# Down products of a two-layer attention and mixture-of-experts kernel: two fp32 passes replaced by three fp32r products of leading and trailing parts

## What is computed

```python
xn = ln(x, g_norm)
q = (xn @ Wq) ; k, v = split(xn @ Wkv)        # 16 heads of 64, one k/v head
q, k = l2norm(q) * q_scale, l2norm(k) * k_scale
attn = softmax(q @ k.T * 8 + bias, causal, masked)   # bias of a small network, plus a null key
x = x + ln(attn @ v @ Wout, g_out)

scores = softmax((x @ wt.T + g @ wg.T) / 2)   # 8 experts, the best 2 are kept, weights sum to 1
gp = leaky(x @ w_gate) ; up = x @ w_up         # per expert, 128 hidden units
y_all = (gp * up) @ w_down                     # per expert: the down products
y = sum of the two chosen y_all, weighted
p = (leaky(x @ sw_gate) * (x @ sw_up)) @ sw_down    # shared, 256 hidden units
x = x + y + p
```

## Time and profile before

| | |
|---|---|
| device time, 3 runs | 1133.45, 1135.3, 1136.15 us (median 1135.3) |
| device time of the profiled execution | 1139.32 us |
| its span, first to last instruction | 1137.4 us |
| TensorE matmul busy | 1028.3 us (90%), 7340 instructions |
| VectorE busy | 781.0 us (69%) |
| ScalarE busy | 526.0 us (46%) |
| GpSimd busy | 443.3 us (39%), 422 instructions |
| down products (L1460) | 640 instructions, mean 395 ns |
| granted TensorE clock, mean | 0.976 |
| round 4 (its expert transposes to the next ones) | 425.7 to 556.3 us |
| the tail | 1078.2 to 1137.4 us |

### The profile page before, as it was taken

The page is one execution under the profiler, slowest core; times in us unless marked ns, Lnnn a source line. Parts: engine busy times, 40 slices in busy tenths (PEclk is TensorE's granted clock), DMA queues, the critical chain, the costliest instruction groups (busy, mean ns, idle before and its releaser), DMA issues.

```text
span 1137.4 us, 22612 instructions
## 1 busy us (share of the span) xinstructions
PE 1028.3 (90%) x7340; PEld 843.4 (74%) x7340; DVE 781.0 (69%) x2538; ACT 526.0 (46%) x1563; POOL 443.3 (39%) x422
## 2 busy tenths in 40 slices
PE   2377899999999999899999999899998999999898
PEld 1265587777877788677877787777877778777777
DVE  6768858775687648775587747876597756866442
ACT  2048724663356614655255623565146642566111
POOL 3154414553435505453336424354145433355112
PEclk9688999999999999999999999999999999999999
DMA  5064411321123212321123111221113211232033
GB/s 203 19 177 158 150 38 56 104 85 57 40 80 98 66 40 74 103 66 38 58 91 96 59 55 58 92 68 65 59 56 103 84 38 33 81 103 65 20 104 119
DMA packets 40939, 89.89 MB, mean 79 GB/s; under 512 B 4128, under 2 KB 18976, under 8 KB 40304
## 3 DMA queue, kind: packets, MB, share of 16 engines
q1 hardware_dynamic: 40816, 88.29, 24.3%
HBM read 78.67 MB, written 11.70 MB: 79 GB/s over the span
## 4 chain that ended last, share of the span: by engine, by line
PE 66%; DVE 20%; issue 6%; ACT 5%; POOL 1%; DMA 1%; SPq 1%; DVEq 0%; ACTq 0%; POOLq 0%
PE psY L1460 11%; PE psO L1393 6%; PE psS L1363 5%; PE psG L63 4%; PE psG L65 4%; PE psG L64 4%; PE psT L1374 3%; PE psS L63 3%; PE psS L64 3%; DVE work L1042 3%; PE psS L65 3%; PE psS L1358 2%; PE psO L1396 2%; PE psT L63 2%; PE psT L65 2%
## 5 line engine op out<-in xcount | busy, mean ns | idle before, releaser
L552 POOL TENSOR_TENSOR work<-work,rden 128x514 f32<-128x514 f32 x128 | 134.3, 1049 | 329.1 <-DVE rden L1023 328.5
L1460 PE MATMUL psY<-Wd,H 128*128 128x256 f32 x640 | 166.7, 395 | 3.7 <-POOL H L566 3.7
L675 ACT ACTIVATE work<-work,low 128x257 f32<-128x257 f32 x256 | 128.3, 503 | 80.7 <-DVE low L1042 80.6
L63 PE MATMUL psG<-x1T_hi,Wgu 128*128 128x512 f32 x280 | 128.1, 458 | 11.7 <-ACT leaky L707 9.8
L1460 PEld LDWEIGHTS psY<-Wd,H 128*128 128x128 f32 x640 | 113.3, 189 | 32.3 <-issue 15.6
L1042 DVE CUSTOM_DVE_ANT_0 work<-psS,bias,null_s 128x256 f32<-128x256 f32 x256 | 113.0, 478 | 18.3 <-PE psS L1363 18.0
L1132 DVE SCALAR_TENSOR_TENSOR leaky<-leaky 128x512 f32<-128x512 f32 x80 | 55.6, 695 | 101.5 <-ACT leaky L707 100.5
L541 POOL TENSOR_TENSOR rq<-qss,neghalf 128x16 f32<-128x16 f32 x32 | 93.7, 2930 | 55.0 <-DVE qss L1017 55.0
L65 PE MATMUL psG<-x1T_lo,Wgu 128*128 128x512 f32 x280 | 110.3, 394 | 0.0
L64 PE MATMUL psG<-x1T_hi,Wgu 128*128 128x512 f32 x280 | 109.6, 391 | 0.0
L667 ACT ACTIVATE qT_hi<-psO 128x256 fp32r<-128x256 f32 x128 | 48.9, 382 | 108.8 <-PE psO L1396 107.7
(11 more groups left out here) (242 smaller groups left out, 2677.4 us busy)
## 6 DMA issues: line engine op xcount, KB each, us to landing
Wgu<-wexp SPq DMA_DIRECT2D x80, 512.0 KB, 3.5
Wb<-wscr SPq DMA_DIRECT2D x64, 256.0 KB, 3.7
wexp<-Wgu SPq DMA_DIRECT2D x10, 512.0 KB, 2.9
xin<-in_x SPq DMA_DIRECT2D x8, 512.0 KB, 4.1
xres<-in_x SPq DMA_DIRECT2D x8, 512.0 KB, 5.0
out<-work SPq DMA_DIRECT2D x8, 512.0 KB, 3.1
H<-in_wgu SPq DMA_DIRECT2D x10, 256.0 KB, 3.8
bscr<-bscr SPq DMA_DIRECT2D x1, 2048.0 KB, 13.0
```

The costliest lines, as they stand in the source:

```text
L63: te.matmul(dst, a_hi, b_hi, start=start, stop=False)
L552: pool.tensor_tensor(T1[sl][:, hs, :], T1[sl][:, hs, :], rden[sl][:, 1, hs].unsqueeze(2) .to_broadcast([P, 2, N + 1]), ALU.mult)
L675: act.activation(T1[sl][:, h, :], T1[sl][:, h, :], ACT.Exp, scale=-1.0, bias=low[sl][:, 1, h:h + 1], accum_out=den[sl][:, 1, h:h + 1])
L1460: mm = te.matmul(psY[:, t // 2, (t % 2) * D:(t % 2 + 1) * D], H[:, k % H_RING, t * P:(t + 1) * P], Wd[:, ORDER[k], :], start=(k == 0 and t ...
```

## The change

Each down product becomes three: leading by leading, trailing by leading, leading by trailing part. `Wd` is split once, in round 0: its four pieces are loaded behind the third expert weights into buffers that are free then (`wd_in`), ScalarE writes the leading parts and GpSimd subtracts for the trailing ones (`DOWN_SPLIT_AT`). `H` is split for each block: ScalarE's `lead` copies it to a leading part and GpSimd's `trail` subtracts; both write into `Hp`, a ring of two in the buffers of the transposed tokens `xnT`, which hold nothing in use then. `lead(k)` waits for the weighted (or shared) hidden values and for the down products of block k - 2; `trail(k)` for `lead(k)`; `down(k)` and the reuse of `H` for `trail(k)`. The down products of blocks 0 and 1, which stood ahead of step 0, go to steps 1, 3 and 4, and block 2 wholly into step 5. `WT` moves into unused rows of `PNT`, so the product with `PNT` takes 64 rows.

```diff
-DOWN_AT = {4: (2, FIRST), 5: (2, SECOND), 6: (3, FIRST), 7: (3, SECOND), 8: (4, WHOLE), 9: (5, FIRST), 10: (5, SECOND),
-           11: (6, FIRST), 12: (6, SECOND), 13: (7, FIRST), 14: (7, SECOND), 15: (8, FIRST), 16: (8, SECOND), 18: (9, WHOLE)}
+LEAD_AT = {3: 2, 4: 3, 5: 4, 7: 5, 9: 6, 11: 7, 13: 8, 15: 9}
+TRAIL_AT = {3: 2, 4: 3, 5: 4, 7: 5, 9: 6, 11: 7, 13: 8, 15: 9}
+DOWN_AT = {1: (0, WHOLE), 3: (1, FIRST), 4: (1, SECOND), 5: (2, WHOLE), 6: (3, FIRST), 7: (3, SECOND), 8: (4, WHOLE),
+           9: (5, FIRST), 10: (5, SECOND), 11: (6, FIRST), 12: (6, SECOND), 13: (7, FIRST), 14: (7, SECOND),
+           15: (8, FIRST), 16: (8, SECOND), 18: (9, WHOLE)}
+HP_RING = 2
+DOWN_PARTS = 4
+DOWN_SPLIT_AT = {7: 0, 9: 1, 10: 2, 11: 3}
...
+        wd_in = [(range(0, 4), Wb[:, :, :].rearrange("p b t -> p (b t)")), (range(4, 6), leaky[0][:]),
+                 (range(6, 8), leaky[1][:]), (range(8, 10), x1[:, 0:2, :].rearrange("p t d -> p (t d)"))]
...
 @block.sync
-            sp.dma_start(Wd[:], wdown).then_inc(ld_down.sem, 16)
...
             for e in range(BLOCKS + 2):
+                if e == H_RING:
+                    for blocks, raw in wd_in:
+                        sp.dma_start(raw, wdown[:, blocks[0]:blocks[-1] + 1, :].rearrange("p b d -> p (b d)")) \
+                            .then_inc(ld_down.sem, 16)
...
 @block.gpsimd (attention)
                     if t < POOL_TILES:
                         scale_q(pool, r, t, qn_pool)
+                    if t == 3 and moe is not None:
+                        trail(moe, 0)
+                        trail(moe, 1)
                 for n in range(ALL):
+                    if moe is not None and n in TRAIL_AT:
+                        trail(moe, TRAIL_AT[n])
                     if moe is not None and n in WEIGH_AT:
                         weigh(moe, WEIGH_AT[n])
+                    if moe is None and n in DOWN_SPLIT_AT:
+                        blocks, raw = wd_in[DOWN_SPLIT_AT[n]]
+                        hi, lo = (part[:, blocks[0]:blocks[-1] + 1, :].rearrange("p b d -> p (b d)") for part in Wd)
+                        pool.wait_ge(wd_lead.sem, DOWN_SPLIT_AT[n] + 1)
+                        pool.tensor_tensor(lo, raw, hi.bitcast(F32), ALU.subtract).then_inc(wd_trail.sem, 1)
...
+            def trail(m, k):
+                need(pool, hh_done, m, k + 1)
+                pool.tensor_tensor(Hp[1][:, k % HP_RING, :], H[:, k % H_RING, :], Hp[0][:, k % HP_RING, :].bitcast(F32),
+                                   ALU.subtract).then_inc(hl_done.sem, 1)
...
 (GpSimd's tail)
-            for k in range(SHARED, BLOCKS):
-                weigh(ROUNDS - 1, k)
+            for k in range(BLOCKS):
+                if k >= SHARED:
+                    weigh(ROUNDS - 1, k)
+                if k >= 1:
+                    trail(ROUNDS - 1, k - 1)
+            trail(ROUNDS - 1, BLOCKS - 1)
...
 @block.scalar (attention)
+                if moe is not None:
+                    lead(moe, 0)
                 for n in range(4):
                     turned_q(r, n)
                     if n == 1 and moe is not None:
                         take_gate(moe, 2)
+                        lead(moe, 1)
...
+                    if moe is not None and n in LEAD_AT:
+                        lead(moe, LEAD_AT[n])
+                    if moe is None and n in DOWN_SPLIT_AT:
+                        blocks, raw = wd_in[DOWN_SPLIT_AT[n]]
+                        act.wait_ge(ld_down.sem, 16 * DOWN_PARTS)
+                        act.activation(Wd[0][:, blocks[0]:blocks[-1] + 1, :].rearrange("p b d -> p (b d)"), raw,
+                                       ACT.Copy).then_inc(wd_lead.sem, 1)
                     if TURN_LAG <= n < ALL + TURN_LAG:
                         turned(r, n - TURN_LAG)
...
+            def lead(m, k):
+                if k < SHARED:
+                    need(act, h_done, m, k + 1)
+                else:
+                    need(act, hw_done, m, k + 1 - SHARED)
+                if k >= HP_RING:
+                    need(act, h_used, m, k + 1 - HP_RING)
+                act.activation(Hp[0][:, k % HP_RING, :], H[:, k % H_RING, :], ACT.Copy).then_inc(hh_done.sem, 1)
...
 (ScalarE's tail)
             for k in range(BLOCKS):
                 take_gate(ROUNDS - 1, k, True)
+                if k >= 2:
+                    lead(ROUNDS - 1, k - 2)
+            lead(ROUNDS - 1, BLOCKS - 2)
+            lead(ROUNDS - 1, BLOCKS - 1)
...
 @block.vector (hidden)
-                    need(dve, h_used, m, k + 1 - H_RING)
+                    need(dve, hl_done, m, k + 1 - H_RING)
...
 @block.tensor
                 if moe is not None:
                     up(moe, 2)
-                    down(moe, 0, WHOLE)
-                    down(moe, 1, WHOLE)
...
             def down(m, k, tiles):
-                if k < SHARED:
-                    need(te, h_done, m, k + 1)
-                else:
-                    need(te, hw_done, m, k + 1 - SHARED)
+                need(te, hl_done, m, k + 1)
...
-                    mm = te.matmul(psY[:, t // 2, (t % 2) * D:(t % 2 + 1) * D],
-                                   H[:, k % H_RING, t * P:(t + 1) * P], Wd[:, ORDER[k], :],
-                                   start=(k == 0 and t % 2 == 0), stop=(k == BLOCKS - 1), skip_group_check=True)
+                    for a, b in ((0, 0), (1, 0), (0, 1)):
+                        mm = te.matmul(psY[:, t // 2, (t % 2) * D:(t % 2 + 1) * D],
+                                       Hp[a][:, k % HP_RING, t * P:(t + 1) * P], Wd[b][:, ORDER[k], :],
+                                       start=(k == 0 and t % 2 == 0 and a + b == 0), stop=(k == BLOCKS - 1 and b == 1),
+                                       skip_group_check=True)
```

More of the change, by code:

```diff
@@ L140, in attention_moe @@
         Wout = [sb(f"Wout_{part}", [P, PAIRS, D], F32R) for part in PARTS]
-        Wd = sb("Wd", [P, BLOCKS, D])
+        Wd = [sb(f"Wd_{part}", [P, BLOCKS, D], F32R) for part in PARTS]
         Wt = sb("Wt", [P, KC, E])
@@ L202, in attention_moe @@
         Wb = sb("Wb", [P, WB_RING, TOK])
-        WT = sb("WT", [E, TOK])
+        Hp = xnT
+        WT = PNT[DH:DH + E, :]
         lg = sb("lg", [P, TILES, E])
@@ L352, in attention_moe @@
         hw_done = events("hw_done", E, 1)
+        hh_done = events("hh_done", BLOCKS)
+        hl_done = events("hl_done", BLOCKS)
+        wd_lead = events("wd_lead", 0)
+        wd_trail = events("wd_trail", 0)
         xnT_ps = events("xnT_ps", 2)
@@ L1342, in attention @@
                                  [part[:, p, :] for part in Wout], p == 0, False)
-                    te.matmul(dst, PNT[:, t * P:(t + 1) * P], Unull[:], start=False, stop=True) \
+                    te.matmul(dst, PNT[0:NULL_ROWS, t * P:(t + 1) * P], Unull[0:NULL_ROWS, :], start=False, stop=True) \
                         .then_inc(wo_ps.sem, 1)
@@ L1470, in _ @@
             te.wait_ge(w_trail.sem, 2)
-            te.wait_ge(ld_down.sem, 16)
             keys(0)
@@ L1474, in _ @@
             attention(0, None, 1)
+            te.wait_ge(wd_trail.sem, DOWN_PARTS)
             with te.Fori(1, ROUNDS - 1) as r:
```

5 lines of the change are left out of this document (3 added, 2 removed).

## The result

| | before | after |
|---|---|---|
| device time, median of 4 runs | 1134.38 us (1133.03 to 1136.15) | 1179.93 us (1179.89 to 1180.26) |
| profiled execution, span | 1139.32, 1137.4 us | 1179.89, 1177.8 us |
| program's start to the first expert transposes (round 0) | 165.0 | 173.3 |
| rounds 1 to 7 | 913.2 | 931.0 |
| tail | 59.2 | 73.5 |

What follows compares the result with a forecast made beforehand. The bound was priced by stage: TensorE in mid-round, VectorE's chain at round entries. TensorE -7, entries +13, step 11 +6, round 0 +4 and tail +13 made +29 on 1139.3; 1168 less 4 gave 1164 us, range 1150 to 1176.

Steps and rivals of the forecast that it cites:

- Direction: Whole kernel: the change makes it slower, chance 0.92.
- the tail (+13): Last token block's experts: down(1) waits 5.5 us, six periods grow from 4.46 to 5.7 us; +13 us (10 to 16).
- Entry of each round (+1.9): Seven round entries: two GpSimd subtractions hold off VectorE's router operations, +1.9 us each (0 to 2.1), +13 us in all.
- Nothing is gained there ... Price zero: Moving downs 0 and 1 from ahead of step 0 into steps 1, 3 and 4 neither gains nor costs.
- Step 11 (+0.9): VectorE's norm_x is held off by one more subtraction, placed in front: +0.9 us (0 to 1.2), six rounds, +6 us.
- TensorE's part from step 5 on (-1.0): Three down products replace two fp32 instructions: 1.0 us less a round (0.3 to 1.8), seven rounds, -7 us.
- Round 0 (+4): Splitting Wd loads ScalarE and GpSimd, and its loads delay the fourth expert-weight load: +4 us (1 to 7).
- less 4: Whole kernel: 4 us off the sum, since unprofiled runs' median is 4.0 us below the profiled execution.
- one subtraction only: Round entry: only one subtraction is in VectorE's way, 0.95 us a round, giving 1157 us; chance 0.15.
- no hold-off: Rounds: subtractions into fp32r tiles run beside VectorE without stopping it, giving 1145 us; chance 0.12.
- TensorE is the bound and the copies are hidden: Whole kernel, tail included: faster, 26 us less than 1135, giving 1109 us; chance 0.05.
- the clock falls in the tail: Tail: the stall before down(1) brings half clock speed for some 7 us more, giving 1171 us; chance 0.10.

Runs made afterwards that it cites:

- a_tail: Changed kernel, in the tail each subtraction ahead of the next block's weighting and each leading copy right behind the gate copy, one block earlier: 1167.3 us, ratio 1.0303.
- a_down_first2: Changed kernel, down products of blocks 0 and 1 ahead of step 0 again, block 2 still whole in step 5: 1174.3 us, ratio 1.0361.
- b_down_later: Kernel before, its fp32 down products of blocks 0 and 1 moved into steps 1 and 3, no copies or subtractions: 1141.6 us, ratio 1.0073.
- b_rows64: Kernel before, only the null product narrowed from 128 to 64 rows: 1147.4 us against 1135.4, ratio 1.0117.
- best5: Changed kernel, 128-row null product, downs 0 and 1 ahead of step 0, entry, step-11, tail and round-0 copies or subtractions rescheduled, down(7) whole in step 14: 1134.4 us, ratio 0.9991.
- a_rows128: Changed kernel, null product over all 128 rows again: 1173.2 us, ratio 1.0355.
- b_turn: Kernel before, the tail's routing weights transposed right behind gate(1) and copied behind the first gate copy: 1134.2 us, ratio 0.9991.
- a_round0_late: Changed kernel, Wd's loads behind the eighth expert-weight load and its split in steps 12 to 15 of round 0: 1175.4 us, ratio 1.0384.

## Why the prediction was wrong, point by point

- **Direction, and the tail (+13):** right. +14.3 in the profile, with period and place of down(1) as worked out; the last down ends 69.3 us into the tail (forecast 68.2). a_tail confirms the order as its cause. What the sum lacked is the first period, 7.16 us for 5.61, with the half-clock stretch in it.
- **Entry of each round (+1.9):** the mechanism and the size were right: 2.0 us, by a_down_first2. Missed was what TensorE does in that time.
- **"Nothing is gained there ... Price zero" for the downs of blocks 0 and 1:** this step failed. It asked only whether score(0) would come earlier, not what the idle that takes the place of 3.5 us of products does to the clock. It costs 0.3 to 0.5 us a round with a half-clock stretch of 3.4 us and 1.0 to 1.9 with one of 6.8, some 5 us together; b_down_later shows 8.2 us for the move alone. I had the clock as a rival in the tail, where the earlier trace rows showed it, and did not carry it to the place where the change made a new wait.
- **The null product over 64 rows:** the step that is missing, and the largest. The text on the change named it; the prediction put it at nothing, without a reason. By b_rows64 it is 12 us in the kernel before (10.4 to 16 by the interval); in the changed kernel the traces place 9.2 us.
- **Step 11 (+0.9):** the size was right: score(12) to score(13) takes 6.1 us after and 5.2 before; best5 takes it back. The order was misread: the subtraction comes behind the two normalization instructions. The size came out because norm_x is held off by a subtraction behind them as by one in front.
- **TensorE's part from step 5 on (-1.0):** about right: in round 1, score(5) to score(15) less step 11's 0.9 is 0.8 shorter, and from score(15) to the round's end a_rows128, without the narrow product, is 0.4 shorter in the mean of rounds 1 to 6 than the kernel before: 1.2 a round. Round 7 gives 3, of it 1.5 by a slow end in the trace of the kernel before (b_turn's end is that much shorter). The pitch is 0.12 as read from the earlier trace rows.
- **Round 0 (+4):** +8.3, of it 1.5 the null product. The queue was as forecast (a load of 7.3 us, ScalarE waits 1.94); the rest was under-sized. a_round0_late gives 4 to 7 us back. Round 0 also has four half-clock stretches of 3.4 us between 90 us and its end where the kernel before has one; no run separates what they cost.
- **"less 4":** the profiled execution of the kernel before is 4.9 us above its median; that of the changed kernel lies at its median (1179.89). 3.5 us of the excess sat in rounds 4 to 6, whose score(0) came at 28.3 us instead of 27.1. Single rounds of other kernels show the same shift (one of b_rows64, one of b_turn, two of a_tail), the profiled changed kernel has none; what makes it was not tested. Subtracting it from the sum took off what the changed kernel does not have. That is 4 us of the 16.

So, against the sum: round 0 +4.3, of it 1.5 the null product; rounds 1 to 7 +5.8, which is 7.7 for the null product and 4.9 for what a_down_first2 takes back, less 3.5 that the kernel before loses by itself in rounds 4 to 6 and some 3 by which TensorE's part came out shorter than forecast; tail +1.3; and 4 for the offset.

The rivals: *one subtraction only* fell (both operations waited); *no hold-off* fell; *TensorE is the bound and the copies are hidden* fell (the periods of the tail are longer, TensorE waits for the subtraction in each); *the clock falls in the tail* was right in kind: the half-clock stretch behind the wait for down(1) goes with a first period 1.55 us longer than the next ones, where I had put 7 us. The larger place of the clock was the entries.
